# Cross-attention of a decoder layer: the first batch's probabilities and values as one f32 array in place of two f16 parts

## What is computed

```python
q = (x @ Wq.T).reshape(b, t, 32, 8)         # 16 heads, two halves each
k = (ctx @ Wk.T).reshape(b, 77, 32, 8)
v = (ctx @ Wv.T).reshape(b, 77, 16, 16)
lam = exp(sum(lq1 * lk1)) - exp(sum(lq2 * lk2)) + 0.8
att = softmax(q @ k / sqrt(8))              # per half
out = (att[first halves] - lam * att[second halves]) @ v
x = layernorm(x + out)
```

## Time and profile before

| what | value |
|---|---|
| median of three runs | 885.98 us (884.12 to 889.12) |
| the profiled execution, from first to last instruction | 886.2 us |
| TensorE matmul busy | 86% |
| VectorE busy | 70% |
| ScalarE busy | 50% |
| GpSimd busy | 38% |
| mean granted TensorE clock | 0.946 of full speed |

### The profile page before, as it was taken

One profiled execution on the slowest core, in us unless ns is written; L12 is line 12 of the kernel. 1 busy time (PEld: TensorE's weight loads), 2 busy tenths in 40 slices (PEclk: granted clock), 3 DMA queues, 4 the chain that ended last, 5 costly groups with the idle time before them and its releaser, 6 DMA issues.

```text
span 886.2 us, 24076 instructions
## 1 busy us (share of the span) xinstructions
PE 765.4 (86%) x9352; PEld 519.2 (59%) x9352; DVE 619.9 (70%) x1605; ACT 441.9 (50%) x904; POOL 332.5 (38%) x368
## 2 busy tenths in 40 slices
PE   5889989988898998877989987998678898799972
PEld 2466656655566664545657654666556787576541
DVE  8777755577777866977677777467868557853676
ACT  5777755345674533466453434652135665464321
POOL 6221212012891210399511114530444454256663
PEclk9999999999999999999889989998989998899987
DMA  8355574040000002011200031152565324223452
GB/s 294 121 180 160 123 156 123 1 148 1 25 3 1 1 2 61 28 48 36 84 2 1 2 108 47 43 200 97 207 193 151 104 88 128 77 88 100 150 186 75
DMA packets 57701, 80.77 MB, mean 91 GB/s; under 512 B 15096, under 2 KB 45944, under 8 KB 57080
## 3 DMA queue, kind: packets, MB, share of 16 engines
q1 hardware_dynamic: 50936, 62.71, 23.5%
q0 software_dynamic: 5376, 15.47, 4.8%
q10 hardware_dynamic: 1280, 1.05, 0.5%
HBM read 42.65 MB, written 33.41 MB: 86 GB/s over the span
## 4 chain that ended last, share of the span: by engine, by line
PE 53%; DVE 25%; ACT 9%; issue 4%; POOL 4%; SPq 2%; DMA 2%; ACTq 1%; DVEq 0%
PE ps L1624 27%; PE ps L1630 9%; PE ps L1722 4%; PE ps L1738 3%; DVE xmax L1482 3%; PE ps L1703 2%; DVE st L1273 2%; DVE rows L1290 2%; ACT qk L1035 1%; PE ps L1847 1%; SPq L740 1%; DVE xrec L1501 1%; ACT square L1038 1%; PE ps L1766 1%; POOL prob L949 1%
## 5 line engine op out<-in xcount | busy, mean ns | idle before, releaser
L942 POOL TENSOR_TENSOR qk<-square,qk 128x512 f16<-128x512 f32 x64 | 77.2, 1206 | 359.7 <-ACT qk L1041 359.7
L1630 PE MATMUL ps<-attn_mem 128*64 128x65 f32 x1920 | 95.8, 225 | 3.0 <-DVE state L1446 1.6
L1624 PE MATMUL ps<-x_split,w_qkv 128*128 128x512 f16 x384 | 95.0, 384 | 1.2 <-ACT attn_mem L1044 1.2
L971 POOL DMA_INDIRECT rows_out<-attn_mem,dest x64 | 62.6, 978 | 79.0 <-ACT attn_mem L1155 65.5
L1630 PEld LDWEIGHTS ps<-attn_mem 128*64 128x64 f32 x1920 | 85.5, 140 | 4.4 <-issue 2.5
L1427 DVE SCALAR_TENSOR_TENSOR qk<-ps,qk 128x512 f16<-128x512 f32 x64 | 44.1, 688 | 45.5 <-ACT square L1038 45.3
L1035 ACT ACTIVATE qk<-ps 128x512 f16<-128x512 f32 x64 | 38.3, 598 | 74.4 <-PE ps L1624 74.4
L964 POOL DMA_INDIRECT rows_in<-rows,slot_i x48 | 47.8, 995 | 51.1 <-DVE slot_i L1363 39.5
L1624 PEld LDWEIGHTS ps<-x_split,w_qkv 128*128 128x128 f16 x384 | 33.2, 98 | 48.1 <-issue 12.1
L1049 ACT ACTIVATE attn_mem<-ps 128x512 f32<-128x512 f32 x64 | 34.7, 594 | 51.7 <-PE ps L1722 51.7
L1624 PE MATMUL ps<-attn_mem,w_qkv 128*128 128x128 f16 x512 | 57.8, 230 | 1.2 <-DVE attn_mem L1554 1.1
(11 more groups left out here) (315 smaller groups left out, 2027.0 us busy)
## 6 DMA issues: line engine op xcount, KB each, us to landing
attn_mem<-rows_in SPq DMA_DIRECT2D x64, 144.0 KB, 2.4
late_mem<-ffn_w SPq DMA_DIRECT2D x17, 384.0 KB, 4.2
rows_in<-zero_row SPq DMA_DIRECT2D x32, 144.0 KB, 2.7
up_split<-late_mem SPq DMA_DIRECT2D x16, 256.0 KB, 2.7
x_stage<-xT SPq DMA_DIRECT2D x4, 512.0 KB, 5.6
down_split<-late_mem SPq DMA_DIRECT2D x16, 128.0 KB, 3.0
rows<-x SPq DMA_DIRECT2D x4, 512.0 KB, 5.2
xq<-late_mem SPq DMA_DIRECT2D x32, 64.0 KB
```

The source lines that it names most:

```text
L942: pool.tensor_tensor(parts[:, 3, :], square[:, n % 2, :], parts[:, 2, :], ALU.subtract).then_inc(p_sql.sem, 1)
L971: pool.indirect_dma_start(rows_out[b], bass.IndirectOffsetOnAxis(ap=dest[:, i % YB, j:j + 1], axis=0), yb[:, i % YB, j, :], None).then_inc ...
L1624: ins = pe.matmul(dst, lhs(i), rhs(j), start=first and n == 0, stop=last and n == 2)
L1630: ins = pe.matmul(dst[at:at + COLS, :], lhs[:, at:at + COLS], rhs, start=start, stop=stop)
```

## The change

Blocks 0 and 1 take the form of blocks 2 and 3. `WIDE` goes, `prob` and `xv` are f32 arrays of the same bytes, and `prob_full` stays only as memory for other stages (`stage_mem`). The casts, the second exponential and GpSimd's subtract go with their semaphores. The product of the reciprocals with lambda's coefficients (L1501) is as it was. No constant of the schedule changes.

The arrays:

```diff
-        xv = sb("xv", [P, NG, GC, 2, GV], F16)
+        xv = sb("xv", [P, NG, GC, GV])
...
-        prob = sb("prob", [P, RING, 2, TB], F16)
-        prob_full = sb("prob_full", [P, FULL, TB])
+        prob = sb("prob", [P, RING, TB])
+        stage_mem = sb("stage_mem", [P, STAGED, TB])
```

The SP queue, the parts of the values:

```diff
-                        if b == 0:
-                            for part in range(2):
-                                value_parts.append((
-                                    xv_scr[r % P:r % P + rows, :, r // P, part, cols],
-                                    v_ext[n0:n0 + rows, part, :, :].rearrange("n (g i) d -> n g i d", i=2)[:, :, j // 2, :]))
-                        else:
-                            value_parts.append((
-                                xv_wide_scr[r % P:r % P + rows, :, r // P, cols],
-                                v_wide[n0:n0 + rows, :, :].rearrange("n (g i) d -> n g i d", i=2)[:, :, j // 2, :]))
+                        value_parts.append((
+                            xv_scr[b, r % P:r % P + rows, :, r // P, cols],
+                            v_ext[b][n0:n0 + rows, :, :].rearrange("n (g i) d -> n g i d", i=2)[:, :, j // 2, :]))
```

GpSimd, "probs":

```diff
-                elif kind == "probs" and b < WIDE:
-                    if high_on_act(n):
-                        pool.wait_ge(*pr_exp(b, n + 1))
-                    else:
-                        pool.wait_ge(*pr_high(0, highs_on_dve(b, n)))
-                    pool.tensor_tensor(prob[:, n % RING, 1, :], prob_full[:, n % FULL, :], prob[:, n % RING, 0, :],
-                                       ALU.subtract).then_inc(pr_low.sem, 1)
```

ScalarE, "probs":

```diff
-                elif kind == "probs" and b < WIDE:
-                    act.wait_ge(*pr_done(b, n + 1))
-                    if high_on_act(n):
-                        if n >= RING:
-                            act.wait_ge(*weighed(b, 2 * (n // GC - 1)))
-                        act.activation(prob[:, n % RING, 0, :], bank[:, :], ACT.Exp, scale=float(XD) ** -0.5)
-                    if b or n >= FULL:
-                        act.wait_ge(*pr_low(0, CHUNKS * b + n - FULL + 1))
-                    if b and n < FULL:
-
-                        act.wait_ge(*sd_done(b - 1, 2))
-                    act.activation(prob_full[:, n % FULL, :], bank[:, :], ACT.Exp,
-                                   scale=float(XD) ** -0.5).then_inc(pr_exp.sem, 1)
                 elif kind == "probs":
                     act.wait_ge(*pr_done(b, n + 1))
                     if n >= RING:
                         act.wait_ge(*weighed(b, 2 * (n // GC - 1)))
-                    act.activation(prob_wide[:, n % RING, :], bank[:, :], ACT.Exp, scale=float(XD) ** -0.5
+                    act.activation(prob[:, n % RING, :], bank[:, :], ACT.Exp, scale=float(XD) ** -0.5
                                    ).then_inc(pr_exp.sem, 1)
```

VectorE, "probs":

```diff
-                elif kind == "probs" and b < WIDE and not high_on_act(n):
-                    dve.wait_ge(*pr_exp(b, n + 1))
-                    if n >= RING:
-                        dve.wait_ge(*weighed(b, 2 * (n // GC - 1)))
-                    dve.tensor_copy(prob[:, n % RING, 0, :], prob_full[:, n % FULL, :]).then_inc(pr_high.sem, 1)
```

TensorE, "weigh":

```diff
-                        pe.wait_ge(*(pr_low(0, CHUNKS * b + GC * (g + 1)) if b < WIDE else pr_exp(b, GC * (g + 1))))
+                        pe.wait_ge(*pr_exp(b, GC * (g + 1)))
                     for c in (2 * half, 2 * half + 1):
                         for chunk in range(GC):
-                            if b >= WIDE:
-                                last = by_columns(bank[:, GV * c:GV * c + GV],
-                                                  prob_wide[:, (GC * g + chunk) % RING, P * c:P * c + P],
-                                                  xv_wide[:, g, chunk, :], chunk == 0, chunk == GC - 1)
-                                continue
-                            last = three_pass(
-                                bank[:, GV * c:GV * c + GV],
-                                lambda i: prob[:, (GC * g + chunk) % RING, i, P * c:P * c + P],
-                                lambda j: xv[:, g, chunk, j, :], chunk == 0, chunk == GC - 1)
+                            last = by_columns(bank[:, GV * c:GV * c + GV], prob[:, (GC * g + chunk) % RING, P * c:P * c + P],
+                                              xv[:, g, chunk, :], chunk == 0, chunk == GC - 1)
```

More of the change, by code:

```diff
@@ L43 @@
 LAG = 4
-FULL = 3
+STAGED = 3
 MAX_SCALE = 64.0
@@ L398, in decoder_layer @@
         sh_w = sb("sh_w", [P, 2, FW], F16)
-        hid_s = prob_full[:, 0, :]
-        hT_s = prob_full[:, 1, :].bitcast(F16).rearrange("p (a t) -> p a t", a=2)
+        hid_s = stage_mem[:, 0, :]
+        hT_s = stage_mem[:, 1, :].bitcast(F16).rearrange("p (a t) -> p a t", a=2)
         ge = sb("ge", [P, NT * NE])
@@ L454, in decoder_layer @@
         xq_stage = xq[:, :, :].rearrange("p g t -> p (g t)").bitcast(F32)
[L455 to L456 removed]
+        full_stage = stage_mem[:, :, :].rearrange("p r t -> p (r t)")
+        prob_mem = prob[:, :, :].rearrange("p r t -> p (r t)")
         kb_hl = prob_mem[:, 0:4 * GN].bitcast(F16).rearrange("p (n a c) -> p n a c", n=2 * B, a=2)
@@ L463, in decoder_layer @@
         VEXT = XV * (XV + 1)
-        v_ext = acc_mem[:, 0:VEXT].bitcast(F16).rearrange("p (a h d) -> p a h d", a=2, h=XV)
-        v_wide = acc_mem[:, VEXT:VEXT + XV * (XV + 1)].rearrange("p (h d) -> p h d", h=XV)
+        v_ext = [acc_mem[:, VEXT * b:VEXT * b + VEXT].rearrange("p (h d) -> p h d", h=XV) for b in range(B)]
         kb_full = x_mem[:, 0:GN].rearrange("p (j n) -> p j n", j=GH)
@@ L734, in setup @@
                     sp.wait_ge(*kb_low(0, 2 * B))
-                    sp.wait_ge(*v_copied(0, 6))
+                    sp.wait_ge(*v_copied(0, 2 * B))
                     sp.wait_ge(*zero_stored(0, B))
@@ L756, in _ @@
             sp.wait_ge(*zeros_v(0, 1))
-            sp.dma_start(xv_scr, xv[:, :, :, :, :]).then_inc(zero_stored.sem, 16)
-            sp.dma_start(xv_wide_scr, xv_wide).then_inc(zero_stored.sem, 16)
+            for b in range(B):
+                sp.dma_start(xv_scr[b], xv[:, :, :, :]).then_inc(zero_stored.sem, 16)
             for n in (7, 8):
@@ L1202, in setup @@
                 if s == 0:
-                    dve.memset(v_ext[0:CTX, 0, :, XV:XV + 1], 1.0).then_inc(v_copied.sem, 1)
-                    dve.memset(v_ext[0:CTX, 1, :, XV:XV + 1], 0.0).then_inc(v_copied.sem, 1)
-                    dve.memset(v_wide[0:CTX, :, XV:XV + 1], 1.0).then_inc(v_copied.sem, 1)
+                    for b in range(B):
+                        dve.memset(v_ext[b][0:CTX, :, XV:XV + 1], 1.0).then_inc(v_copied.sem, 1)
                     dve.wait_ge(*xkv_done(0, 1))
-                    v_full = [banks[VALUE_BANK][0:CTX, D * b:D * b + D].rearrange("p (h d) -> p h d", d=XV) for b in range(B)]
-                    dve.tensor_copy(v_ext[0:CTX, 0, :, 0:XV], v_full[0]).then_inc(v_copied.sem, 1)
-                    dve.wait_ge(*v_copied(0, 4))
-                    dve.tensor_tensor(v_ext[0:CTX, 1, :, 0:XV], v_full[0], v_ext[0:CTX, 0, :, 0:XV],
-                                      ALU.subtract).then_inc(v_copied.sem, 1)
-                    dve.tensor_copy(v_wide[0:CTX, :, 0:XV], v_full[1]).then_inc(v_copied.sem, 1)
+                    for b in range(B):
+                        v_full = banks[VALUE_BANK][0:CTX, D * b:D * b + D].rearrange("p (h d) -> p h d", d=XV)
+                        dve.tensor_copy(v_ext[b][0:CTX, :, 0:XV], v_full).then_inc(v_copied.sem, 1)
                     dve.wait_ge(consts.sem, CONSTS)
@@ L1634, in _ @@
             free[KEY_BANK] = [kb_low(0, 2 * B)]
-            free[VALUE_BANK] = [v_copied(0, 6)]
+            free[VALUE_BANK] = [v_copied(0, 2 * B)]
             expert_of = {}
```

25 lines of the change are left out of this document (5 added, 20 removed).

## The result

The changed kernel takes 863.6 us in the median of four runs (863.45 to 867.47), the kernel before beside it 887.55 (884.12 to 889.81): a ratio of 0.974, interval 0.971 to 0.977. In two later sets, each on a chip of its own, the same pair gave 0.980 (0.974 to 0.985) and 0.977 (0.972 to 0.983). The forecast was 871.4 us, range 865 to 879. The profiled execution of the changed kernel spans 861.7 us and took 863.45; the forecast had put span and time as one, so against its sum stands the span: 871.6 forecast, 861.7 found.

The account below looks back on a forecast made before the run. TensorE, busy 86%, was taken as the bound, plus its idle time and halved clock. 14.5 idle + 6.5 clock - 7.0 added work + 0.6 setup = 14.6 us off 886.2 gives 871.6, so 871.4 as median; range 865 to 879.

Parts of the forecast that it names:

- Idle time given back: TensorE's waits in and just ahead of block 0's and 1's cross-attention stretches shrink: 14.5 us gained, bounds 5 and 18.
- I leave 1.1 us as it is: Per stretch, TensorE's 0.7 us wait for L1504 and some shorter ones stay, since L1501 stood behind the remaining subtract L942.
- Clock given back: In the two cross-attention stretches, TensorE's half-clock time after waits comes back: 6.5 us of 9.1 missing, ends 0 and 9.1.
- TensorE's work added: 48 f32 matmuls replace 36 f16 ones: 0.44 us more in each of 16 groups, 7.0 us lost, all on the path.
- ScalarE behind TensorE: From chunk 6 on, exponentials wait 0.44 us longer for the group two before; costed at nothing, 3.2 us if cover goes.
- Setup: SP stores 61 parts, not 67; steps 13 and 14 later, step 15 shorter: +0.6 us gained, ends -3 and +2.
- GpSimd itself is idle most of the time: Claim that removing 48 subtracts, 57.0 us of GpSimd, helps TensorE's path only through the waits named, not through GpSimd's load.
- The hold on L1501: VectorE's L1501 stands still until GpSimd's queue of subtracts has a gap: 1563 ns average in block 1's stretch, 252 in block 2's.
- Rival A: L942 and scatters keep blocking L1501: 4 us idle per stretch instead of 1.1, 877.2 us; A or B together 0.22.
- Rival B: In the two stretches the remaining waits still halve TensorE's clock, 6.5 us stay lost: 877.9 us; A or B together 0.22.
- Rival C: ScalarE's exponentials, waiting for weighed groups, delay feature copies TensorE needs: up to 25.6 us lost, 897 us; chance 0.03.
- Rival D: Gain is small, lower ends together: 887 us, no change; waits had another cause than L949 and the casts; chance 0.05.

Follow-up runs that it names:

- e4: Kernel before with one f16 exponential per chunk, no casts or subtracts, 36 f16 matmuls per group, low part left out: 864.1 us, ratio 0.9765.
- e3: Changed kernel with ScalarE's 24 first exponentials put back into a spare buffer: 863.4 us, ratio 0.9739 to the kernel before.
- e8: Kernel before with GpSimd's subtract cut to 8 of 512 columns, signals kept, low part left out: 895.6 us against 914.1 in its set.
- e1: Changed kernel with GpSimd's 48 subtracts put back, nobody waiting for them: 872.4 us, ratio 0.9856 to the kernel before.
- e10: Changed kernel with VectorE's 24 casts put back into an unread buffer, no subtracts: 867.4 us against the changed kernel's 868.0 in its set.
- e2: Changed kernel with GpSimd's 48 subtracts and VectorE's 24 casts put back, nobody waiting for them: 879.0 us, ratio 0.9917 to the kernel before.
- e9: Kernel before with GpSimd waiting for its own previous subtract before each one, leaving queue gaps: 881.5 us against 885.2 in its set.

## Why the forecast fell short

**The ground of the argument held.** The idle time of the two stretches, the clock lost in them, TensorE's added work and setup each have the sign forecast. Against the working, for the first pair of profiles:

- *Idle time given back*: 14.5 forecast, 16.5 found (8.3 to 3.5 and 14.2 to 3.5 inside the stretches, with 1.0 ahead of them). What was mis-sized is "I leave 1.1 us as it is": 0.5 to 0.6 stayed, though VectorE is still held 0.9 to 1.0 us behind the remaining subtract. The norm's 3.4 us also went to 3.0; e4, with f16 products, keeps 3.4. The 1.0 ahead of the stretches is exact; e3 shows it.
- *Clock given back*: 6.5 forecast, 8.3 found in the stretches by e4's reading. The deduction of a fifth for idle time was too much.
- *TensorE's work added*: -7.0 forecast, -7.5 found (twice 49.95 - 46.2, the idle rest of a halved clock included). These three make 17.3; the milestones above say 17.0. The row of 1.58 us was right (1.57 measured); the estimate of 1.52 by the Trainium skill, "FP8 and Floating Point Precision", section "TensorE Precision Notes", was 0.05 too low.
- *ScalarE behind TensorE*: 0 forecast, 0 found; no wait of TensorE for an exponential inside either stretch.
- *Setup*: +0.6 forecast, 1.8 in this pair, 2.4 and 0.2 in the two others. I set the later steps 13 and 14 against the shorter step 15. The rows of after have 4.28 us for step 13, where the half-width parts took 5.17, and 7.45 for step 14 against 5.09: 1.5 us later in all and not the 3.8 that I set against the gain.
- *Outside the stretches*: nothing forecast, 5.7 found in this pair. **This is the step that failed**: "clock given back" was taken for the two stretches alone, with 0 at all other places and no reason given. It is the largest part of the 9.9 us by which the span misses the sum; idle time and clock in the stretches make 3.0 and setup 1.2, errors of size only. With the other terms at what they measured (17.0 + 1.8 = 18.8) the span would be 867.4, some 869 as a time, inside the range.

Only half of the 5.7 repeats. The three pairs have 5.7, 2.9 and 0.3 us outside: in each, 2.9 are the half-clock pieces at 600 and 610 us, which the old kernel has and the changed one has not, for a cause that stays open; the remainder comes and goes, and in the first pair it fell to the side of the changed kernel. That the time lies below the range rather than just inside it is in part this luck: the spans of the later pairs differ by 19.1 and 17.9 us in place of 24.5, which is a gain inside the range's 7 to 21.

**The causes.** That the subtracts were behind the waits was right (e8), but two of the reasons were not. "GpSimd itself is idle most of the time" is an average: in block 1's stretch its subtracts, adds, scatters and indirect DMAs come to 51 us, and e1 shows that this bulk alone makes the stretch 6.8 us longer through the adds in front of the norm. And the casts, which I named beside the subtracts, cost nothing by themselves (e10); they cost only beside subtracts (e2). The hold on L1501, on which I put the argument, is real (e9 shortens it by gaps alone), but its price is not shown. With gaps in the queue and with nobody waiting for the results, e1 and e2 put back 6.8 and 8.3 of block 1's 13.3 us. The other 5.0 us (7.2, as e1 and e2 have the f32 products that make a stretch 2.2 us longer) divide in a way that no run shows between holds over several instructions and the waits of TensorE and ScalarE for the subtracts' results; e9, where TensorE waits 4.6 us for them, says that the second is not small.

Rival A named the right place (the remaining subtract does hold the product, 0.93 us where nothing holds it for 0.17) with a price some seven times too high: TensorE lost 0.5 to 0.6 us per stretch, not 4. Rival B fell: with the norm's wait and 0.6 us left, both stretches have 0.99 to 1.00. Rival C had nothing behind it. Rival D fell with e8.

## What to carry to other kernels

A queue that is 38% busy over a kernel can be the bound of one stretch: read its busy time in the window where it matters, and ask which of its later instructions others wait for. Where VectorE instructions of a known size take several times their length, look at what GpSimd runs back to back beside them. A short gap between such instructions shortens the hold, but it also delays their results: count the waits for those too. And TensorE's clock can differ between two executions of one kernel at places that a change does not touch, by some 3 us of time here: before trusting a term for it, or a difference found there, take more than one profile of each kernel.

## What the runs showed of the hardware

- GpSimd's subtracts with no gap between them hold a VectorE instruction with two SBUF inputs through all of them: 3.40 us before, 4.10 us in e2, for work of 0.17 us. With a gap of 0.14 us it gets in at the first gap (e9). The Trainium skill, "SBUF — State Buffer", section "Who interferes with whom", says that the first to issue has the shared ports for its whole instruction and the other blocks. The runs agree for a single instruction (0.93 us beside a subtract that ends at 403.06) and show more: the one that waits is passed over when the next instruction of the holder follows at once.
- A VectorE cast from f32 to f16 within SBUF is lengthened by the same neighbours: 454 ns alone, 833 on average beside the subtracts.
- The issue of an indirect DMA on GpSimd does not hold the product by itself. In the changed kernel and in e10 products start within such an issue and take 0.17 us; the product, then GpSimd, in e10:

```profile
400.03 0.17 DVE L1455 TENSOR_TENSOR xrec<-xrec,coef 128x16 f32<-128x16 f32 x1
```

```profile
399.37 0.99 POOL L936 DMA_INDIRECT rows_in<-rows,slot_i  x1 [0.15 <-issue]
```

- The products that are held through an issue (1.90 us in e9, 4.10 in e2) have a subtract right behind it, and there the hold begins up to 0.7 us before that subtract's start in the profile. Why is open.
- TensorE's clock behind one and the same wait can be 1.2 GHz in one execution and 2.4 in the next: 15 and 32 matmuls in 3 us behind norm2 of block 0.
